# Gather indices of the first four groups read straight from memory, and the start-up loads issued from two queues, in a four-layer graph network on one core

## What is computed

```python
edge_index = jnp.stack([src, dst])
x = _layernorm(x + _L0_gnn_ref(x, src, dst, ...))          # two GAT layers
x = _layernorm(x + _L1_gnn_ref(x, edge_index, W, b))       # mean over the edges into a node
x = _layernorm(x + _L2_gnn_ref(x, edge_index, edge_attr, ...))  # edge MLP; mean, max and sum
x = _layernorm(x + _L3_gnn_ref(x, edge_index, W, att, bias))    # GAT layer with one head
# in _L0_gnn_ref:
feat = (x @ W).reshape(num_nodes, H, D)
e = jax.nn.leaky_relu(el[src] + er[dst], NEG_SLOPE)
msg = feat[src] * alpha[:, :, None]
rst = jax.ops.segment_sum(msg, dst, num_segments=num_nodes)
```

## Time and profile before

| | |
|---|---|
| median of 3 runs | 2471.84 us (2467.99 to 2473.29) |
| profiled execution, its own time | 2472.98 us |
| its span in the profile | 2471.2 us |
| PE busy | 1932.7 us, 78% |
| DVE busy | 1718.3 us, 70% |
| POOL busy | 1380.7 us, 56% |
| ACT busy | 1118.5 us, 45% |
| mean granted clock of TensorE | 0.674 of full speed |

### The profile page before, as it was taken

The page is one execution under the profiler, slowest core; times in us unless marked ns, Lnnn a source line. Parts: engine busy times, 40 slices in busy tenths (PEclk is TensorE's granted clock), DMA queues, the critical chain, the costliest instruction groups (busy, mean ns, idle before and its releaser), DMA issues.

```text
span 2471.2 us, 32119 instructions
## 1 busy us (share of the span) xinstructions
PE 1932.7 (78%) x7888; PEld 1297.1 (52%) x7888; DVE 1718.3 (70%) x6541; ACT 1118.5 (45%) x3061; POOL 1380.7 (56%) x1388
## 2 busy tenths in 40 slices
PE   3999998974777778847755665999995899959883
PEld 2888988873664223336645654566563222235552
DVE  6444444448775887669968896799895566678773
ACT  0322222223665556625535554566664555524332
POOL 4777777740002667700037773377666777727776
PEclk9655556665556777755558786999998555556555
DMA  4555555535224567624449775343531999923441
GB/s 149 168 154 154 155 157 158 156 130 199 107 107 145 168 174 208 189 79 149 150 132 245 214 214 160 93 130 129 168 119 62 315 367 316 308 80 104 127 138 29
DMA packets 268830, 401.92 MB, mean 163 GB/s; under 512 B 94344, under 2 KB 110881, under 8 KB 268517
## 3 DMA queue, kind: packets, MB, share of 16 engines
q1 hardware_dynamic: 217684, 311.07, 38.6%
q0 software_dynamic: 43904, 75.95, 11.6%
q10 hardware_dynamic: 7056, 12.85, 1.4%
HBM read 222.04 MB, written 185.39 MB: 165 GB/s over the span
## 4 chain that ended last, share of the span: by engine, by line
POOL 16%; DVE 13%; issue 11%; ACT 8%; PE 3%; DMA 2%; POOLq 0%; SPq 0%; DVEq 0%; ACTq 0%
POOL ring L659 8%; POOL out_dram L665 4%; POOL big L659 4%; ACT outr L721 4%; DVE stats L675 4%; DVE G L1149 3%; ACT big L1794 2%; DVE mv L684 1%; DVE z L1521 1%; DVE z L1864 1%; DMA ring<-x_t,idx 1%; ACT big L1802 1%; ACT hT L1780 1%; DVE z L1673 1%; PE bank L1537 0%
## 5 line engine op out<-in xcount | busy, mean ns | idle before, releaser
L659 POOL DMA_INDIRECT ring<-in_x_dram,idx x392 | 379.3, 968 | 147.4 <-issue 118.9
L721 ACT ACTIVATE outr<-z,rn 128x128 f32<-128x128 f32 x784 | 322.6, 483 | 301.2 <-DMA out_dram<-outr,idx 111.5
L659 POOL DMA_INDIRECT ring<-x_t,idx x280 | 268.5, 959 | 304.6 <-SPq L303 210.3
L659 POOL DMA_INDIRECT ring<-hidden_e,idx x196 | 193.6, 988 | 313.8 <-DVE idx L1403 256.8
L665 POOL DMA_INDIRECT x_t<-outr,idx x196 | 234.3, 1195 | 160.7 <-ACT outr L721 114.9
L1149 DVE TENSOR_TENSOR_SCAN G<-cont,G,bank 64x512 f32<-64x512 uint8 (+1 forms) x192 | 240.6, 1253 | 37.6 <-PE bank L1227 32.4
L665 POOL DMA_INDIRECT out_dram<-outr,idx x196 | 194.3, 991 | 103.1 <-issue 58.5
L1925 PE MATMUL bank<-DB,z 20*128 20x512 f32 x196 | 201.3, 1128 | 22.8 <-DVE outr L1379 7.0
L1021 DVE BATCH_NORM_STATS2 stats<-ring 128x6 f32<-128x128 f32 x196 | 42.8, 281 | 247.2 <-DMA ring<-in_x_dram,idx 247.1
L1227 PE MATMUL bank<-ident,msg 128*64 128x128 f32 (+1 forms) x588 | 151.9, 412 | 73.9 <-DVE msg L1134 71.0
L1537 PEld LDWEIGHTS bank<-W_s,G 65*128 65x128 f32 (+1 forms) x784 | 163.9, 308 | 64.7 <-issue 62.2
(11 more groups left out here) (383 smaller groups left out, 4577.1 us busy)
## 6 DMA issues: line engine op xcount, KB each, us to landing
hT<-in_x_dram SPq DMA_DIRECT2D x194, 256.0 KB
x_t<-outr SPq DMA_DIRECT2D x98, 256.0 KB, 2.9
ring<-x_e SPq DMA_DIRECT2D x98, 256.0 KB, 4.3
x_t<-xload SPq DMA_DIRECT2D x48, 512.0 KB, 3.5
xsrc_e<-ring SPq DMA_DIRECT2D x49, 256.0 KB, 2.6
xd_e<-ring ACTq DMA_DIRECT2D x49, 256.0 KB, 2.7
ring<-xsrc_e SPq DMA_DIRECT2D x49, 256.0 KB, 3.5
x_t<-xT SPq DMA_DIRECT2D x49, 256.0 KB, 4.0
```

The lines of the kernel that those rows point to most:

```text
L659: nc.gpsimd.indirect_dma_start(to(c), None, table, bass.IndirectOffsetOnAxis(ap=idx[:, kind, (g + 1) * GT + c:(g + 1) * GT + c + 1].bitcas ...
L721: ins = nc.scalar.activation(to[:, k, :], frm[:, k, :], ACT.Identity, bias=sc[:, k, 1:2], scale=sc[:, k, 0:1])
```

## The change

Three things change, and all of them are in the preparation and at the start of stage a.

- ACT, as its first work, issues two new DMAs that write `idx[:, SRC, 4:20]` and `idx[:, DST, 4:20]`, which are the indices of groups 0 to 3, straight from `src` and `dst` in memory. In memory the numbers of one partition lie 128 apart, so a DMA moves 2,048 single elements of 4 bytes. They count up the new semaphore `idx0`.
- POOL waits for `idx0` before the first gather, and for `torow` only before the first gather of group 4. DVE no longer clears or writes `idx[:, 0..1, 4:20]`, and waits for `idx0` before it makes `dlo`, `dhi` and `shi`.
- The nine edge loads and the 26 other loads are split over two queues. SP issues the first four edge loads and every second one of `loads`; ACT issues the other five and the other 13, behind the two new ones.

```diff
+        def prep_loads(eng, half):
+            eng.wait_ge(S("pads"), 1)
+            for to, frm in (edges[:4], edges[4:])[half]:
+                eng.dma_start(to, frm).then_inc(S("edges"), 16)
+            for to, frm in loads[half::2]:
+                eng.dma_start(to, frm).then_inc(S("weights"), 16)
+
         def prep_sync(sp):
...
-            for to, frm in edges:
-                sp.dma_start(to, frm).then_inc(S("edges"), 16)
-            for to, frm in loads:
-                sp.dma_start(to, frm).then_inc(w, 16)
-            prep_sync.loads = len(loads)
-
+            prep_loads(sp, 0)
             sp.wait_ge(S("srclo"), 1)
@@
-            c.do(v.memset(idx[:], 0))
+            c.do(v.memset(idx[:, :, 0:GT], 0))
+            c.do(v.memset(idx[:, :, GT + NT:], 0))
@@
-                to = to.rearrange("p (q r) -> p r q", r=2)
-                v.tensor_copy(to, bank[m % 2][:, 0:2 * P].rearrange("p (r q) -> p r q", r=2)[:, :, 0:NQ]) \
+                q0 = RING * GT // 2 if m < 2 else 0
+                to = to.rearrange("p (q r) -> p r q", r=2)[:, :, q0:]
+                v.tensor_copy(to, bank[m % 2][:, 0:2 * P].rearrange("p (r q) -> p r q", r=2)[:, :, q0:NQ]) \
                     .then_inc(S("torow"), 1)
@@
+            v.wait_ge(S("idx0"), 32)
             for n, kind, op, by in ((0, DST, ALU.bitwise_and, P - 1), (1, DST, ALU.logical_shift_right, 7),
@@
         def prep_scalar(a):
+            for n, frm in ((SRC, src), (DST, dst)):
+                a.dma_start(idx[:, n, GT:GT + RING * GT], frm[0:RING * GE].rearrange("(c p) -> p c", p=P),
+                            allow_slow_non_contiguous=True) \
+                    .then_inc(S("idx0"), 16)
+            prep_loads(a, 1)
             a.wait_ge(S("b1min"), 1)
@@
         def a_pool(pool):
             def step(i, j):
                 g = RING * i + j
+                if g == 0:
+                    pool.wait_ge(S("idx0"), 32)
+                if g == RING:
+                    pool.wait_ge(S("torow"), 2)
                 need(pool, "a_tr", g + 1 - RING)
@@
             arrive(pool)
-            pool.wait_ge(S("torow"), 2)
             a_pool(pool)
```

More of the change, by code:

```diff
@@ L386, in program @@
         PREP_DVE = {name: n + 1 for n, name in enumerate(['ends', 'links', 'tomake', 'biasc', 'attb', 'bcols'])}
-        def prep_sync(sp):
[L389 to L416, removed]
-            for to, frm in edges:
-                sp.dma_start(to, frm).then_inc(S("edges"), 16)
-            for to, frm in loads:
-                sp.dma_start(to, frm).then_inc(w, 16)
-            prep_sync.loads = len(loads)
@@ new lines, in program @@
+        loads = [
+            (W1x[:, 0:HF], W1), (W2_s[0:HF, :], W2), (W2_s[HF:HF + 1, :], rowof(b2)), (raw, L1W),
+            (M1a[:], M1[0:F, :]), (M1b[:], M1[F:F + EF, :]), (M2_s[:], M2), (Mm_s, Mm), (Mx_s[:], Mx),
+            (Ms_s, Ms), (W3_s[:], W3),
+            (bias[:, 0, :], b2.partition_broadcast(P)), (bias[:, 1, :], L1b.partition_broadcast(P)),
+            (bias[:, 2, :], bm.partition_broadcast(P)), (bias[:, 3, :], b4.partition_broadcast(P)),
+            (bload[:, 0, :], bx.partition_broadcast(P)), (bload[:, 1, :], bs.partition_broadcast(P)),
+            (alb[:, 0, 0:HF], al1.rearrange("h d -> (h d)").partition_broadcast(P)),
+            (alb[:, 0, HF:], ar1.rearrange("h d -> (h d)").partition_broadcast(P)),
+            (hT[0:HF, 0, 0, 0:F], al2.rearrange("h d -> (h d)").partition_broadcast(HF)),
+            (hT[0:HF, 0, 1, 0:F], ar2.rearrange("h d -> (h d)").partition_broadcast(HF)),
+            (b1c[:, 0:1], col(b1)), (m1c[:], col(m1)), (m2c[:], col(m2)),
+            (attc[:, 0:1], col(att[0, 0:F])), (attc[:, 1:2], col(att[0, F:])),
+        ]
@@ new lines, in program @@
+        edges = [
+            (e_src[0:FULL, :], src[0:FULL * CH].rearrange("(q c) -> q c", c=CH)),
+            (e_src[FULL:FULL + 1, 0:REST], rowof(src[FULL * CH:E])),
+            (e_dst[0:FULL, :], dst[0:FULL * CH].rearrange("(q c) -> q c", c=CH)),
+            (e_dst[FULL:FULL + 1, 0:REST], rowof(dst[FULL * CH:E])),
+            (e_prev[0:1, 1:CH], rowof(dst[0:CH - 1])),
+            (e_prev[1:FULL, :], dst[CH - 1:FULL * CH - 1].rearrange("(q c) -> q c", c=CH)),
+            (e_prev[FULL:FULL + 1, 0:REST + 1], rowof(dst[FULL * CH - 1:E])),
+            (e_next[0:FULL, :], dst[1:FULL * CH + 1].rearrange("(q c) -> q c", c=CH)),
+            (e_next[FULL:FULL + 1, 0:REST - 1], rowof(dst[FULL * CH + 1:E])),
+        ]
@@ L423, in prep_sync @@
+        LOADS, ELOADS = len(loads), len(edges)
+        def prep_loads(eng, half):
[4 more added lines that the diff above has]
+                eng.dma_start(to, frm).then_inc(S("weights"), 16)
+        def prep_sync(sp):
+            prep_loads(sp, 0)
             sp.wait_ge(S("srclo"), 1)
@@ L512, in prep_vector @@
             v.memset(e_prev[0:1, 0:1], -1).then_inc(S("pads"), 1)
-            c.do(v.memset(idx[:], 0))
+            c.do(v.memset(idx[:, :, 0:GT], 0))
+            c.do(v.memset(idx[:, :, GT + NT:], 0))
             v.wait_ge(S("shapes"), 8)
-            v.wait_ge(S("edges"), 16 * 9)
+            v.wait_ge(S("edges"), 16 * ELOADS)
             for n, t in ((0, e_src), (1, e_dst), (8, e_prev), (9, e_next)):
@@ L643, in prep_scalar @@
         def prep_scalar(a):
+            for n, frm in ((SRC, src), (DST, dst)):
[3 more added lines that the diff above has]
+            prep_loads(a, 1)
             a.wait_ge(S("b1min"), 1)
             nc.scalar.activation(b1c[:, 3:4], b1c[:, 1:2], ACT.Exp).then_inc(S("b1exp"), 1)
-        LOADS = 26
         def at_tiles(step):
@@ L1983, in _ @@
             prep_sync(sp)
-            assert prep_sync.loads == LOADS
             barrier(sp)
```

## The result

The changed kernel takes 2459.01 us (median of 4 runs, 2454.43 to 2460.3), the kernel before 2472.57 us (median of 4, 2467.99 to 2473.7): a ratio of 0.9944, 95% interval 0.9932 to 0.9957, that is 13.6 us less, with 10.6 to 16.8 as the interval. The profiled execution took 2458.36 us, its span is 2456.6.

The account below looks back on a forecast made before the run. POOL's line of stage a gathers, started late at 31.87 us, was taken as the bound. Starting it earlier gives -15.3, later edges +5.3, together -10.0 us: 2462 us predicted, range 2454 to 2472.

Parts of the forecast that it names:

- The sum: Whole kernel: gather line 15.3 us earlier, less 5.3 us for later edges, gives -10.0 us.
- Step 1: Start of stage a: POOL's first 32 gathers need idx0 alone, start at 8 to 18 us, done at 49 to 59.
- Step 2: Gather 33 waits for its first free ring slot, last for ACT's store xd_e, at 57.8 + d instead of 73.08.
- d: Preparation: how much later the last edge load lands and the preparation ends; taken as 5.3 us, from 1.7 to 9.6.
- Step 3: Edge loads: elements 2.6, passing weights 1.7 and first gathers 1.0 on their one DMA engine delay them by 5.3 us.
- Weights that pass: Edge loads' DMA engine: SP's 13 weight loads may pass ACT's long e_next load, 0 to 3.4 us, taken as 1.7.
- 15.3: Gather 33: us its start moves earlier before d is taken off, 73.08 less 57.8.
- Step 4: Edge and weight loads on two queues: only issue time is saved, no gain, since one DMA engine is the limit.
- Step 5: Preparation: ACT's issues, the weights and DVE's clearing, copies and idx0 wait stay hidden; ACT keeps 18 us of cover.
- Step 6: Stage a: PE starts 15.3 us behind, gains 0.64 a group (9.53 against POOL's 10.17), catches up; whole shift arrives.
- the rival: Stage a: PE can't follow, keeping 10.24 us a group as in turns 34 to 37; 9.4 us later, 2481; 6 in 100.
- the tail of stage a: End of stage a: a fixed tail behind POOL's last gather, where POOL waited 16.6 us at the next barrier.

Follow-up runs that it names:

- index half: Early gathers kept, all edge and weight loads back on SP, against the kernel before: 2458.01 us against 2469.6, ratio 0.9964, on the 2470 us chip.
- control: The kernel before, unedited, run again on the 2470 us chip against its own other runs: ratio 1.0 (0.9991 to 1.0009).
- queue half: Only the loads split over two queues, indices as before, against the kernel before: 2469.33 us against 2469.76, ratio 0.9998, on the 2470 us chip.
- moved stores: ACT, not SP, issues the first four xsrc_e stores; with the 97-row cut on the whole change, 2445.89 us, ratio 0.9906 to the kernel before.
- 96-row edit: Whole change plus each of three 97-row loads cut into 96 rows and 1; alone on the 2920 us chip, ratio 0.997 to the kernel before.

## Why the prediction was right, step by step

**The forecast.** 2462.0 was predicted, with 2454 to 2472, and 2459.01 came. The sum was -10.0 us against a profiled execution; stage a's last gather came 9.5 us earlier in the pair of traces that the sum is about. The medians of the runs are 13.6 us apart, so the time gained more than the sum has; the last part below is about that.

**Step 1, the early gathers.** Gather 1 at 8 to 18: 9.44. The 32 gathers were done by 50.2, ahead of the slot, and cost nothing. Right.

**Step 2, the slot of gather 33, mis-sized by 2.5 us.** I took 57.8 + d, from a store issued at 53.94 and a landing of 2.1 to 5.1 us. The runs have 42.75 us from the cast, 60.3 for a cast at 17.56. The store hung on the preparation as said, and `xd_e` was the last condition as said, by 0.6 us. But this first store, issued at 56.59, lands after 5.4 us (5.2 in the index half), beside six node loads of 256 KB, where the sum has 3.9 with the issue; the landings of the earlier trace rows were mostly of later, quieter ones. And from the landing to the start of the gather it is 0.9 us more, a term that the sum doesn't have. In the kernel before nobody waited for this store, so no row priced either.

**Step 3, d, mis-sized by 2.7 us the other way.** 5.3 was taken, 2.56 measured (2.1 in the index half against its control). The halves tell where: elements and early gathers, 3.6 in my sum, cost 2.13 in the index half. Weights that pass, 1.7 in my sum, cost half a microsecond at most: 0.49 in the queue half against its control, 0.35 between the casts of the index half and the whole change. The elements went in a dense stream and cost less than a column packet in the earlier trace rows. The stretch 2 to 5 us of the changed kernel (packets, their sizes; then queue, packets, MB, share of 16 engines):

```profile
DMA packets 4007, 0.06 MB, mean 20 GB/s; under 512 B 3963, under 2 KB 4007, under 8 KB 4007
...
q10 hardware_dynamic: 4007, 0.06, 84.7%
```

84.7% of 16 x 3 us over 4,007 packets is 10.1 ns each, 44 larger packets included; in the index half the same stretch has 71.3% over 3,941 packets, all but one of them elements, 8.7 ns each. Both are below the 12.3 that I had as the low end. What the early gathers took of the 2.13 no run separates. The two errors nearly cancel: gather 33 is earlier by 15.3 - 2.5 - 2.6 = 10.2 instead of 10.0. That the total was hit so well is luck to that extent. The signs named for this step failed with it: the cast was to start at 22 to 24 and came at 20.12, the preparation was to end at 54 to 56 and ended at 52.2.

**Step 4, two queues.** Right: 0.9998, and the cast is not earlier. In the stretch of 2 to 5 us above, no packet of SP's queue stands at all, though SP issued its first edge load at 2.17; before the change 19 packets had gone by then. In the index half it is one packet, beside 3,940 of ACT's. SP's load started only when nearly all of ACT's elements were through. The Trainium skill (the same page, "Issuing engines are not separate DMA queues") has them interleave; between 5 and 9 us they do (82 packets of SP's queue and 75 of ACT's in the index half), but in these first 3 us the trace shows one behind the other.

**Step 5, what is hidden.** Right in all: no wait of PE, DVE or ACT on a weight appears.

**Step 6, PE follows.** Right that it does, but its own pace was taken for a fixed number, and it goes with the granted clock. Turn 4 was to come at 91 or so and came at 84.20. From turn 2 (70.95) to turn 9 (125.25) PE waited for nobody: 54.3 us for 7 groups, 7.76 a group, where I had 9.53. The stretches from turn 2 to 9 and from turn 7 to 8 of the changed kernel (columns as in the earlier trace rows):

```profile
70.95:125.25 54.30, 54.28 (x366) 50.17 (x365) 29.14 (x197) 19.79 (x49) 41.20 (x44) 0.75 0.63 183
105.62:116.87 11.25, 11.25 (x53) 10.63 (x53) 6.06 (x40) 2.83 (x7) 8.51 (x10) 0.50 0.53 165
```

And the three groups of the rival in the kernel before, turn 34 to 37:

```profile
389.84:420.55 30.71, 30.71 (x156) 28.84 (x157) 14.88 (x101) 7.88 (x20) 23.39 (x25) 0.56 0.52 155
```

A group's time multiplied by the clock is nearly the same in all of them: 7.76 x 0.75 = 5.8, 11.25 x 0.50 = 5.6, 10.24 x 0.56 = 5.7, and the mean of before, 9.53 x 0.61, is 5.8. So the lag was gone after 10 turns, not after 24, since PE had 0.75 in that stretch instead of the mean of 0.61. And the rival's 10.24 was no odd row: it is PE's pace at 0.56, and at 0.50, the 1.2 GHz level, PE takes 11.25, more than POOL's 10.17. What kept the rival away is that the clock was 0.64 on average from turn 4 to turn 48, which at 5.8 makes 9.1 a group; the 438.9 us of that stretch less the 37.0 of waiting are 9.1 a group too. What decides that share I can't tell; PE was as good as always busy both in the stretch at 0.75 and in the one at 0.50.

**What was not foreseen: the last 5 us of the trace.** The span shrank by 14.6 us, stage a only by 9.5. The rest came in stages whose code and inputs are the same in both kernels. The gathers of the third long stage, of the next and of the last one (ns min/median/max, first and last start in us) after the change:

```profile
L667 POOL DMA_INDIRECT ring<-hidden_e,idx x196: 941/946/2653, 772.6 to 1042.3; - x196
L667 POOL DMA_INDIRECT ring<-x_t,idx x280: 940/945/1442, 1252.3 to 2007.3; - x140
L673 POOL DMA_INDIRECT out_dram<-outr,idx x196: 982/985/1522, 2192.4 to 2446.3; - x196
```

The kernel before, in the trace of the prediction:

```profile
L659 POOL DMA_INDIRECT ring<-hidden_e,idx x196: 940/944/2661, 782.7 to 1054.5; - x196
L659 POOL DMA_INDIRECT ring<-x_t,idx x280: 940/944/1455, 1265.7 to 2022.6; - x140
L665 POOL DMA_INDIRECT out_dram<-outr,idx x196: 982/982/1440, 2208.2 to 2460.9; - x196
```

And the same kernel, unchanged, in the control on the 2470 chip:

```profile
L659 POOL DMA_INDIRECT ring<-hidden_e,idx x196: 940/944/2653, 780.4 to 1049.5; - x196
L659 POOL DMA_INDIRECT ring<-x_t,idx x280: 940/944/1447, 1260.6 to 2016.4; - x140
L665 POOL DMA_INDIRECT out_dram<-outr,idx x196: 982/982/1568, 2202.2 to 2456.7; - x196
```

The changed kernel leads the first trace of before by 10.1, 12.2, 13.4, 15.3, 15.8 and 14.6 us at these marks. But the second trace of before leads the first as well, by 2.3, 5.0, 5.1, 6.2, 6.0 and 4.2 us, with no edit at all. Against it the change leads by 7 to 10 us. The third long stage, about which the control was asked, took 271.8 us by its gathers in the first trace, 269.1 in the control and 269.7 in the changed kernel: the long one was the chance. So the excess over 10 us isn't an effect that the change has to have; two executions of one kernel differ by that much. The runs don't exclude a part of it: the result's interval, 10.6 to 16.8, lies above 9.5, and that of the index half, 6.2 to 11.6, does not.

One piece can be told: the tail of stage a, which the forecast took as fixed. The stretches from PE's last turn to the barrier, with the same 60 or 61 matmuls, in the kernel before, in the control and in the index half (columns as in the earlier trace rows):

```profile
532.60:547.00 14.40, 12.72 (x61) 12.63 (x61) 5.02 (x28) 2.77 (x9) 0.00 (x1) 0.50 0.10 38
```

```profile
533.70:544.70 11.00, 9.35 (x60) 9.26 (x58) 3.82 (x22) 3.37 (x10) 0.00 (x0) 0.66 0.09 33
```

```profile
522.20:530.80 8.60, 6.94 (x60) 6.85 (x58) 3.80 (x22) 3.36 (x10) 0.00 (x0) 0.90 0.12 43
```

At a clock of 0.50 it takes 14.4 us, at 0.66 11.0 and at 0.90 8.6, and POOL's wait there 16.6, 14.4 and 12.1. The 2.2 us between the first two waits are as good as the whole lead of 2.3 with which the control enters the third long stage. In the changed kernel the clock was 0.50 there and the wait 16.7, so the tail is no part of its lead over the first trace. What gave the rest, in the later stages, I have not separated.

## What to carry to other kernels

Moving the start of a bound line forward is worth the shift of its first blocked step, not of its first step: look for what the line meets next (here the slot of gather 33) and price the path that frees it, whose transfers nobody waited for until then. Cut a load of 97 rows into 96 and 1 before adding queues: that brought the edges some 12 us forward and, with the second queue and the moved stores, which brought nothing by the marks above, the time 12.1 us below the index half on the same chip. Price the pace of an engine together with the granted clock of the rows from which it is taken. Look at two executions of the same kernel before explaining 0.2% in stages that the edit doesn't touch.

## What the runs showed of the hardware

- Single 4-byte elements, 2 x 2,048 of them from memory, went at 8.7 to 10.1 ns of engine time each, spread over 16 DMA engines: some 3 us in all, and with the early gathers 2.1 us on the load beside them.
- One core program took 2470, 2896 and 2920 us on three chips, with the same issue rate of gathers (0.94 to 0.95 us each) and the same casts up to 20 us; what stretched was the idle time between instructions, in part between two of the same engine. The change is worth 0.5% on one kind of chip and nothing that the runs can tell on the other. With the 96-row edit on top, the whole gives 0.3% (0.05 to 0.56%) against the kernel before on the 2920 chip, and with the moved stores as well 0.8% on the 2896 and 0.9% on the 2470 one.
- The gathers of the third long stage took 271.8 and 269.1 us from first to last in two executions of the same kernel, while the time from the first cast to gather 33 was 42.75 us in three different kernels.
- PE's own pace in stage a was 7.8, 10.2 and 11.25 us a group at granted clocks of 0.75, 0.56 and 0.50, 5.6 to 5.8 us multiplied by the clock.
